# Attention loop of a transformer block: global exponentials later in ScalarE's order, second row maxima one slot later, global rows turned in the values' own PSUM buffer

## The reference

```
def _L0_attn_ref(hidden_states, ...):
    q, k, v = heads(x @ Wq + bq), heads(x @ Wk + bk), heads(x @ Wv + bv)   # 16 heads of 32
    ctx = _local_attention(q, k, v)      # query block of 128 against 256 keys around it
    idx = [0] + top62(norm(q)) + [t - 1] # 64 "global" rows for each head
    g_ctx = softmax(q[idx] @ k.T / sqrt(d)) @ v       # against all 1024 keys
    ctx[idx] = g_ctx
x = x + _layernorm(_L0_attn_ref(_layernorm(x), ...))
x = x + _layernorm(_L0_ffn_ref(_layernorm(x), ...))   # 8 experts of 704, top 1, and a shared one
```

## Time and profile before

| | |
|---|---|
| median of 3 runs | 943.77 us (941.49 to 947.1) |
| profiled execution, its own time | 937.44 us |
| its span, first to last instruction | 935.7 us |
| busy: PE, PEld, DVE, ACT, POOL | 829.6, 672.7, 577.1, 405.0, 139.5 us |
| mean granted TensorE clock | 0.947 |

### The profile page before, as it was taken

One profiled execution on the slowest core, in us unless ns is written; L12 is line 12 of the kernel. 1 busy time (PEld: TensorE's weight loads), 2 busy tenths in 40 slices (PEclk: granted clock), 3 DMA queues, 4 the chain that ended last, 5 costly groups with the idle time before them and its releaser, 6 DMA issues.

```text
span 935.7 us, 13774 instructions
## 1 busy us (share of the span) xinstructions
PE 829.6 (89%) x5060; PEld 672.7 (72%) x5060; DVE 577.1 (62%) x1262; ACT 405.0 (43%) x787; POOL 139.5 (15%) x201
## 2 busy tenths in 40 slices
PE   3999999988888588888868999989999999999994
PEld 2676776766666366666647777769999999887783
DVE  5636994467677254555535876427776666748675
ACT  2523232244554345445554433436666666643020
POOL 4000003020000400111211455110000000003222
PEclk9999999999889797998988999989999999999998
DMA  6696556864565353665121865253777777744534
GB/s 203 180 332 192 167 158 178 263 193 124 162 195 152 105 154 100 198 158 145 49 69 35 263 242 202 94 181 113 223 228 236 236 236 221 230 135 140 187 124 135
DMA packets 117442, 162.38 MB, mean 174 GB/s; under 512 B 17316, under 2 KB 65188, under 8 KB 117376
## 3 DMA queue, kind: packets, MB, share of 16 engines
q1 hardware_dynamic: 113792, 153.54, 53.9%
q0 software_dynamic: 3584, 7.97, 3.0%
HBM read 107.24 MB, written 55.05 MB: 173 GB/s over the span
## 4 chain that ended last, share of the span: by engine, by line
PE 67%; DVE 15%; ACT 6%; DMA 5%; issue 3%; POOL 1%; another core or an unknown queue 1%; SPq 0%; DVEq 0%; POOLq 0%; ACTq 0%
PE bank L163 41%; PE wide L163 18%; PE wide L167 4%; PE bank L167 4%; DVE SG L160 2%; ACT PG L157 2%; DMA H<-scr_oe,FG 2%; DMA scr_v<-vt 1%; DVE MX L160 1%; DVE STC L273 1%; ACT PT L157 1%; DVE CX L1389 1%; DVE CT L149 1%; DMA XX<-scr_h 1%; DVE SIL L149 1%
## 5 line engine op out<-in xcount | busy, mean ns | idle before, releaser
L163 PE MATMUL bank<-XT,W13H 128*128 128x256 f32 (+1 forms) x1056 | 243.0, 325 | 3.1 <-DVE XT L149 3.1
L163 PEld LDWEIGHTS bank<-XT,W13H 128*128 128x128 f32 x1056 | 176.3, 192 | 19.0 <-ACT W13H L145 1.9
L163 PE MATMUL bank<-XT,W13L 128*128 128x256 f32 (+1 forms) x528 | 170.1, 322 | 0.0
L160 DVE TENSOR_REDUCE MX<-wide 128x1 f32<-128x192 f32 (+1 forms) x128 | 77.6, 649 | 73.1 <-PE wide L163 65.9
L163 PE MATMUL wide<-W2H,HH 128*128 128x512 f32 x352 | 117.2, 399 | 3.7 <-DVE CX L1389 3.5
L163 PEld LDWEIGHTS bank<-XT,W13L 128*128 128x128 f32 x528 | 100.9, 191 | 8.1
L163 PEld LDWEIGHTS wide<-W2H,HH 128*128 128x128 f32 x352 | 67.6, 192 | 19.6 <-DVE CX L1389 5.2
L149 DVE TENSOR_TENSOR SIL<-bank,SIL 128x256 f32<-128x256 f32 (+1 forms) x72 | 36.9, 512 | 71.3 <-ACT SIL L157 70.6
L157 ACT ACTIVATE SIL<-bank 128x256 f32<-128x256 f32 (+1 forms) x72 | 32.6, 453 | 109.4 <-PE bank L163 108.5
L163 PE MATMUL wide<-W2L,HH 128*128 128x512 f32 x192 | 76.0, 396 | 0.0
L157 ACT ACTIVATE PT<-bank 128x512 f32<-128x512 f32 x128 | 72.5, 593 | 6.5 <-PE bank L163 5.5
(11 more groups left out here) (205 smaller groups left out, 1539.8 us busy)
## 6 DMA issues: line engine op xcount, KB each, us to landing
R<-in_L_ffn_W_dram SPq DMA_DIRECT2D x48, 512.0 KB, 4.9
scr_q<-hl SPq DMA_DIRECT2D x16, 512.0 KB, 4.3
scr_k<-hl SPq DMA_DIRECT2D x16, 512.0 KB, 3.8
R<-in_L_ffn_sw_dram SPq DMA_DIRECT2D x12, 512.0 KB, 5.0
QSe<-scr_q SPq DMA_DIRECT2D x36, 128.0 KB, 3.1
KSe<-scr_k SPq DMA_DIRECT2D x36, 128.0 KB, 3.4
scr_v<-vt SPq DMA_DIRECT2D x16, 272.0 KB, 2.4
R<-_attn_hidden_states_dram SPq DMA_DIRECT2D x16, 256.0 KB, 3.9
```

Of the source, the lines that this page charges most:

```text
L160: return do("dve", lambda g: g.tensor_reduce(dst, src, AXX, op), after)
L163: return do("pe", lambda g: g.matmul(ps, a, b, start=start, stop=stop, skip_group_check=True), after, mark=mark)
```

## The change

The global exponential is cut off from its maximum and moved from slot 1 to slot 3. The second row maxima of a head move from slot 2 to slot 3, and the top-k part that stood in slot 3 to slot 2. The result of the global values is turned back into columns 512 to 639 of the same double bank that holds the values, so it takes no bank of `ST_`; the double bank is free when VectorE has read the turned rows, no longer when ScalarE has copied the values.

```diff
-            def global_exp(i):
+            def global_max(i):
                 g_ = gp[i]
                 sg = g_["sg"]
                 m_x = red(sg[:, 0:1], g_["w"][:, :], ALU.max, [g_["m_s"]] + g_["sgfree"])
                 g_["m_b"] = ts(sg[:, 1:2], sg[:, 0:1], -SCALE, None, ALU.mult, None, [m_x])
+
+            def global_exp(i):
+                g_ = gp[i]
                 g_["m_e"] = act(g_["pg"][:, :], g_["w"][:, :], ACT.Exp, [g_["m_b"]] + g_["pgfree"],
...
                 m_c = copy("act", os[:, 0:P], w[:, 0:P], [m_o] + sfree)
-                W_.busy[g_["wi"]].append(m_c)
                 g_["os"] = (si, os, m_c)
+                g_["back"] = w[:, 512:512 + P]
...
-                ti, tb, tfree = ST_.take()
-                g_["back"] = (ti, tb)
-                g_["m_t"] = tr(tb[:, 0:P], os[:, 0:P], ident[:, :], [m_c, m_id] + tfree, mark=True)
+                g_["m_t"] = tr(g_["back"], os[:, 0:P], ident[:, :], [m_c, m_id], mark=True)
                 OS.busy[si].append(g_["m_t"])
...
-                ti, w = g_["back"]
+                w = g_["back"]
...
-                ST_.busy[ti].append(halves[1])
+                W_.busy[g_["wi"]].append(halves[1])
...
-            for at, (r, part) in zip([g for g in range(48) if g % 8 in (3, 5, 6, 7)], parts):
+            for at, (r, part) in zip([g for g in range(48) if g % 8 in (2, 5, 6, 7)], parts):
...
-            ROW_MAX = {0: (0, 0), 2: (0, 1), 4: (1, 0), 5: (1, 1)}
+            ROW_MAX = {0: (0, 0), 3: (0, 1), 4: (1, 0), 5: (1, 1)}
...
                 if k == 1 + late and i < 16:
+                    global_max(i)
+                if k == 3 and i < 16:
                     global_exp(i)
```

## The result

The changed kernel took **903.27 us** (median of 4 runs, 900.39 to 904.4), the kernel before 942.63 us beside it (4 runs, 935.35 to 947.1): ratio 0.9585, 95% interval 0.9519 to 0.9651. Two repeats gave 0.9566 (0.9508 to 0.9625; 894.0 against 933.62 us) and 0.9632 (0.9586 to 0.9678; 897.73 against 930.94 us). The forecast was 914.5 us, a ratio of 0.969; the range was 903 to 929. So the time lies at the very edge of the range and outside the 908 to 921 that the forecast called its own, and the gain, 39.4 us, is a third larger than forecast.

What follows compares the result with a forecast made beforehand. TensorE was taken to bound the attention loop, waiting for local exponentials held up by ScalarE's order, with half clock following. Gains 18.0 + 8.0 + 3.1 = 29.1 us took profiled 937.44 to 908.3; timed runs 6.3 higher: 914.5 us, range 903 to 929.

Steps and rivals of the forecast that it cites:

- more than forecast: Rival: row of maxima ready in time and clock full everywhere, 10 us better, 905 us; chance 0.14.
- The row of maxima: Its DMA into the query tile, awaited by the next pair's slot 0 scores: 0.7 us more on the mean, pairs 6 to 14.
- PT wait: TensorE's wait in each pair for the exponentials of the local scores, 1.9 us; claimed to go.
- Row_shift: Transpose of the row maxima in each pair: claimed to start 1.7 us earlier.
- ScalarE behind it: Slot 4's exponential and two copies now come after the global exponential: 0.2 us more a pair.
- The clock's term: Half clock after TensorE's wait, pairs 6 to 14: gone in three pairs of four, 1.2 us less on the mean.
- the clock stays half: Rival: the remaining stops still halve the clock, 13 us come back, 928 us; chance 0.13.
- Pair 0: First pair of the attention loop: its wait goes and a top-k part comes in, about 0.9 us less.
- its 1.23 wait goes: Step for pair 0: TensorE's wait of 1.23 us there disappears.
- Pairs 1 to 5: Pairs where VectorE also runs top-k parts: 1.6 us less each, 8.0 us in all.
- The ends: First and last pair of the loop: about 0.9 us in pair 0 and 2.2 in pair 15, 3.1 us less.
- Pair 6: Pair 11.5 us longer than the rest: its stall was left as it is, outside the sum.

Runs made afterwards that it cites:

- e6: Kernel before, with the value matmuls of slots 0 and 1 done three times to keep TensorE busy in its wait: 914.05 us, 0.9791.
- e1: Kernel before, with only the global exponential moved to slot 3, its maximum staying in slot 1: 891.28 us, 0.9551.
- e4: Changed kernel with the second row maxima put back into slot 2: 898.6 us, 0.9608.
- e2: Changed kernel with the global exponential put back into slot 1, behind its maximum: 916.06 us, 0.9793.
- e5: Changed kernel with the top-k parts of slot 2 put back into slot 3: 890.51 us, 0.9556.
- e3: Changed kernel with the turned global rows put back into a bank of the score ring: 895.43 us, 0.9588.
- e7: Changed kernel with the value loads moved from slot 2 to the end of slot 5 in even pairs: 896.56 us, 0.959.
- e9: e5 with the DMA of the row of maxima issued from ScalarE's queue instead of SP's: 905.72 us, 0.9723.

## Why the prediction was right, and where its sizes were off

The path was right, and the size came out at the place of a rival. 903.27 us is where "more than forecast" (905, chance 0.14) put it, and the trace shows that rival's condition in most pairs: row ready in time and clock full in 7 to 9 and 11 to 14. By the earlier trace rows, e6 and the changed kernel the 138.50 us of pairs 7 to 14 split up as follows. Without the half clock they take 127.50 (e6), 1.4 us a pair less (forecast 1.2). Without the wait eight pairs of 14.4 take 115.2, another 1.5 (forecast 1.7 - 0.2 = 1.5). The row of maxima, with the half clock behind it, gives 0.4 back (forecast 0.7). That is 2.5 us a pair against 2.0, and more than half of the difference is the row of maxima.

1. **The mechanism held.** The PT wait went, and GC took its place at 0.88 us (forecast 1.0). Row_shift starts 1.72 us earlier (1.7). The term "ScalarE behind it" was 0.2 and comes out at 0.2 by difference: without any half clock, a pair with the wait takes 15.77 us (e6) and one without it 14.26, which is 1.5 = 1.7 - 0.2. e1 shows that the move of one ScalarE operation does this alone.

2. **The clock's term was too small.** The half clock costs 1.5 us a pair (e6; I read 1.6), and I took 1.2 because I expected it to stay in one pair of four. In pairs 7 to 14 it stayed in one of eight, and that one behind a row wait. So the rival "the clock stays half" was wrong. The row maxima's move, which I had costed only as an inherited wait, seems to be needed for that once the turned rows lie in buffer B (e4, one profile); e1 keeps the clock with neither. My ground for a full clock, pair 0's stop of 1.23 us without a drop, was weak: in e4 stops of the same 1.23 us are followed by a drop in half of the pairs.

3. **The row of maxima was the step with the wrong shape.** I spread 0.7 us over every pair of 6 to 14, most of it in those that load values. It came in pair 10 alone, 1.24 us and a half clock behind it: pair 10 is 17.32 us long and the full-clock pairs 7 to 9 and 11 to 14 are 14.4 on the mean, so 2.9 us once instead of 0.7 nine times. In pair 12 TensorE uses the row 3.3 us after its issue without a stop. The figure from pair 0, 3.85 us, was right for loaded moments only.

4. **Pair 0 had the wrong sign**: forecast 0.9 us less, measured 0.4 more, and 1.0 to 3.2 us more in the other profiles of kernels with the exponential in slot 3 and the row on SP's queue. But e2 and e6, which leave the exponential in slot 1, have 18.6 and 17.1 us too, with waits of 1.5 and 1.4 us for this DMA. The kernel before has one profile, and its 16.0 us may be a low one. The step that failed is "its 1.23 wait goes". Behind that wait TensorE already stood 0.51 us for this DMA; whatever is won in front of it is lost at it, and the issue came no earlier (203.96 in e5 against 203.18), because SP is still issuing head and value loads. A row made earlier only waits there: without a top-k part in front (e1, e4, e5) pair 0 takes 18.1 to 19.2 us, with it (the changed kernel three times, e3, e7) 16.4 to 17.5.

5. **Pairs 1 to 5** gave 8.1 us for a forecast of 8.0, in part by luck. At full clock a pair takes 15.8 us, 1.9 less than before, which is the forecast's figure without a clock loss; I took 0.3 off each for the clock, and one pair (17.95 us, clock 0.90) lost 2.1. In the first repeat none did, and the five gave 10.3. The stop of 1.2 us ahead of row_shift that the moved top-k part makes (forecast 1.3) is there, and e5 shows that it cost 1.0 us a pair that could be had.

6. **The ends.** Busy time of pair 15 and of the expert stage, first of the profile of before, then of after, then of the first repeat:

```profile
470.70:484.40 13.70, 10.12 (x85) 7.04 (x84) 4.27 (x15) 7.07 (x14) 0.55 (x1) 0.88 0.01 2
494.90:935.70 440.80, 415.24 (x2432) 362.09 (x2432) 284.56 (x622) 200.60 (x388) 72.13 (x84) 0.97 0.58 184
```

```profile
435.26:446.20 10.94, 7.47 (x77) 5.43 (x73) 4.29 (x14) 5.88 (x12) 0.55 (x1) 1.00 0.01 2
456.70:901.00 444.30, 417.89 (x2432) 363.97 (x2432) 284.57 (x622) 200.56 (x388) 72.15 (x84) 0.97 0.58 182
```

```profile
428.80:442.60 13.80, 10.58 (x77) 7.37 (x73) 4.30 (x15) 5.88 (x12) 0.55 (x1) 0.75 0.01 2
```

Pair 15 gave 2.8 us (forecast 2.2) where the clock held and nothing in the repeat, with the clock at 0.75. Having no row maxima to do, TensorE stops there 1.75 us for the global exponential, a wait that I had not seen coming. The expert stage, whose 2432 matmuls are the same, took 3.5 us more. In the profiles of all these kernels it is 450 to 460 us from the last step of the global rows to the end, in no order that the edits explain, so single executions differ there by several us. By the start of that stage this profile was 38.2 us ahead (456.7 against 494.9).

7. **Pair 6** gave 7.3 us, where the sum had counted 2.0 as for any pair and had left the stall as it is. The rest isn't shown to be the change's: the same changed kernel has 21.5, 14.9 and 14.9 us there in three profiles, the kernel before 28.8, e1 14.8 and e6 21.7. So the stall comes and goes between executions of one kernel. In the profile after, ScalarE stands idle 2.52 us with nothing named that the core shows, while GpSimd issues its gathers; what it waits for stays open.

The sum against the profile: -0.4 + 8.1 + 7.3 + 20.3 + 2.8 = 38.1, less 3.5 for the expert stage, 34.6 of 34.7. Without pair 6 and the expert stage it is 30.8, against 27.1 of the forecast (29.1 less pair 6's 2.0): 4.3 us more in pairs 7 to 14, 0.1 more in 1 to 5, 0.7 less at the ends. The medians' gain, 33.2 to 39.6 us in the three comparisons, is larger than the forecast by 4 to 10 us. Pair 6's stall, if it is commoner before than after, would explain part of that, but one profile of before can't tell; this stays open.

The version to keep is e1 or e5. e5 took 890.51 us, 3.5 less than the changed kernel beside it, and e1, which needs only the one move, has nearly the same ratio (0.9551 and 0.9556). Both gains over the changed kernel are inside the intervals of the ratios; the pairs 1 to 5 of the traces (73.6 us against 80.8 and, where no clock was lost, 78.6) are the firmer evidence.

## What to carry to other kernels

An engine that works in order should not hold a long operation whose input comes late in front of short ones whose inputs are ready: look for idle time in front of an operation and for others' waits on what stands behind it. Price a TensorE stop with the clock that can fall behind it (here as much again in most pairs), and before counting a gain, look for the wait that already stands next in line, for it takes the gain first. When a loop gets shorter, its small DMAs become the late ones; what stands ahead of them and beside them counts, a store that waits for its data included, and another queue didn't put them first here.

## What the runs showed of the hardware that was not expected

The clock does not follow the length of a stop alone: 1.23 us stops (e4) were followed by half clock in 7 pairs of 14, 1.49 us stops (e2) in none of pairs 7 to 14, and 1.89 us stops (before) in most but not all. What decides was not found. Sixteen matmuls more in each pair made a kernel 19.6 us faster (e6). Of one kind of small DMA, SBUF to SBUF, the time from issue to use was 3.06 us or less ahead of large loads (e5), 3.6 and 4.2 us behind loads on its own queue (pair 10, and pair 0 of e5), and 7.7 us on ScalarE's queue beside them (e9).
